# Attention a projected in narrower pieces, with its values made as token rows, under a new order of work

## What is computed

```
x = x + attn_a(layernorm(x))   # one head of width 128
x = x + ffn(layernorm(x))      # 512 x 512, int4 weights unpacked
x = x + attn_b(layernorm(x))   # 32 heads of width 16, rotary, causal
x = x + ffn(layernorm(x))      # the same weights

attn_a(x): q, k, v = split(x @ Wqkv + bqkv)         # Wqkv is 512 x 384
           a = softmax(q @ k.T / sqrt(128))
           return (a @ v) @ Wo + bo
```

## Time and profile before

| | |
|---|---|
| time, median of 3 runs (range) | 273.23 us (272.33 to 276.82) |
| the profiled execution: its time, its span | 273.97 us, 272.2 us |
| PE busy | 254.4 us, 93% |
| DVE busy | 224.4 us, 82% |
| POOL busy | 182.2 us, 67% |
| ACT busy | 145.0 us, 53% |
| PE's granted clock | 1.000 |

### The profile page before, as it was taken

One profiled execution on the slowest core, in us unless ns is written; L12 is line 12 of the kernel. 1 busy time (PEld: TensorE's weight loads), 2 busy tenths in 40 slices (PEclk: granted clock), 3 DMA queues, 4 the chain that ended last, 5 costly groups with the idle time before them and its releaser, 6 DMA issues.

```text
span 272.2 us, 6539 instructions
## 1 busy us (share of the span) xinstructions
PE 254.4 (93%) x2363; PEld 213.5 (78%) x2363; DVE 224.4 (82%) x402; ACT 145.0 (53%) x239; POOL 182.2 (67%) x229
## 2 busy tenths in 40 slices
PE   7699999998989999999899999997999999999964
PEld 2597887896888987888798898885868876785744
DVE  3682679497798989899888899987988999966976
ACT  2749996644546073457443478526433683268030
POOL 5578978998798495954858587495665552475070
PEclk9999999999999999999999999999999999999999
DMA  7998170203454336334333533531634531102012
GB/s 214 294 392 297 36 198 4 77 2 94 140 147 140 92 91 168 109 88 112 103 113 108 149 94 94 146 107 45 182 111 122 158 87 52 40 3 79 31 68 98
DMA packets 51192, 31.86 MB, mean 117 GB/s; under 512 B 5400, under 2 KB 46552, under 8 KB 51160
## 3 DMA queue, kind: packets, MB, share of 16 engines
q1 hardware_dynamic: 51160, 31.44, 38.8%
HBM read 22.91 MB, written 8.39 MB: 115 GB/s over the span
## 4 chain that ended last, share of the span: by engine, by line
PE 30%; POOL 16%; SPq 15%; DVE 14%; issue 9%; ACT 8%; DMA 7%; DVEq 0%; ACTq 0%; POOLq 0%
SPq L490 13%; PE psum L885 5%; PE psum L886 5%; PE psum L887 5%; PE psum L1052 3%; POOL rstd L543 3%; DVE stats L759 3%; PE psum L1037 3%; DMA QK<-qk_parts 3%; DMA qk_parts<-parts 2%; POOL X L556 2%; DVE XT_lo L764 2%; ACT E L718 2%; PE psum L1015 2%; POOL SH L576 2%
## 5 line engine op out<-in xcount | busy, mean ns | idle before, releaser
L588 POOL TENSOR_SCALAR_AFFINE_SELECT E<-E 128x512 f32<-128x512 f32 x64 | 40.7, 661 | 36.8 <-ACT E L718 36.8
L718 ACT ACTIVATE E<-psum 128x1536 f32<-128x1536 f32 x32 | 46.4, 1449 | 26.3 <-PE psum L1039 19.5
L838 DVE TENSOR_REDUCE nmax<-psum 128x4 f32<-128x512 f32 (+1 forms) x64 | 59.1, 939 | 0.7 <-PE psum L1015 0.6
L885 PE MATMUL psum<-XT_lo,wb_hi 128*128 128x256 f32 x128 | 37.7, 294 | 0.0
L886 PE MATMUL psum<-XT_hi,wb_lo 128*128 128x256 f32 x128 | 36.2, 283 | 0.0
L887 PE MATMUL psum<-XT_hi,wb_hi 128*128 128x256 f32 x128 | 36.1, 282 | 0.0
L622 ACT ACTIVATE XN<-X,offset,rstd 128x512 f32<-128x512 f32 x30 | 24.1, 809 | 19.6 <-POOL offset L544 19.5
L764 DVE TENSOR_TENSOR XT_lo<-psum,XT_hi 128x512 fp32r<-128x512 f32 x32 | 21.5, 683 | 15.6 <-ACT XT_hi L595 15.5
L595 ACT ACTIVATE parts<-SH 128x512 bf16<-128x512 f32 x32 | 19.9, 626 | 25.4 <-POOL SH L581 14.1
L885 PE MATMUL psum<-wb_lo,XT_hi 128*128 128x256 f32 (+1 forms) x96 | 32.6, 339 | 0.0
L1015 PE MATMUL psum<-QK 128*128 128x128 bf16 x256 | 28.8, 220 | 3.1 <-DMA QK<-qk_parts 3.1
(11 more groups left out here) (104 smaller groups left out, 677.5 us busy)
## 6 DMA issues: line engine op xcount, KB each, us to landing
QK<-qk_parts SPq DMA_DIRECT2D x192, 64.0 KB
qk_parts<-parts SPq DMA_DIRECT2D x16, 384.0 KB, 2.8
X<-L_attn_a_x SPq DMA_DIRECT2D x8, 256.0 KB, 4.7
out<-X SPq DMA_DIRECT2D x6, 256.0 KB, 2.4
...
wb_raw<-L_attn_b_wk SPq DMA_DIRECT2D x1, 1024.0 KB, 11.4
wb_raw<-L_attn_b_wv SPq DMA_DIRECT2D x1, 1024.0 KB, 11.9
...
```

The source lines that it names most:

```text
L588: last = nc.gpsimd.affine_select(out=e, in_=e, compare_op=ALU.is_ge, fill=0.0, base=0, pattern=[[0, GH], [1, P]], channel_multiplier=-1)
L718: nc.scalar.activation(E[:, n % 2], bank(3, 3), ACT.Exp, scale=float(HD) ** -0.5).then_inc(done[k], 1)
L838: nc.vector.tensor_reduce(nmax[:, u % 2, g::NG, t], (bank(1, 2) if t else bank(0)).rearrange("p (h k) -> p h k", h=GH), AX, ALU.max, negat ...
L885: nc.tensor.matmul(out_, stat[0], mov[1], start=first, stop=False)
```

## The change

- `Wqkv` comes in three loads of 256 KB: q, k, v. `QH` and `QL` become two steps each, one for q and one for k. The bias of q and k is loaded as two columns, and that of v as 128 channels broadcast to all partitions (`bias_v`), a load of its own.
- Batch 0 is projected by `QP` in six steps instead of `QK` and `QV`: `("QP", t, i)` is token half t of q (i = 0), k (1) or v (2). Each is 4 x 3 = 12 matmuls of 128 moving columns. A step needs only its own half of the tokens and its own part of the weight.
- `QV` for batches 1 to 3 now takes the tokens as the stationary operand and the v weight as the moving one: 2 x 4 x 3 = 24 matmuls of 128 columns. `QK` stays as it was for those batches.
- `VC`, `VA` and `AC` are gone. A new DVE step `VB` reads the product in PSUM, adds the bias row and writes `va`, which has two slots.
- `PLAN` is a new list throughout, and 9 `KP` matmuls stand at the start instead of 14. All steps not named here are the same in kind and number.

The list, its beginning only:

```diff
-    ("D", "x", 0, 1), ("LN", 1, 0, 1), ("D", "x", 0, 0), ("D", "x", 1, 0), ("D", "x", 1, 1), ("RS", 1, 0, 1),
-    ("KP", 14), ("NO", 1, 0, 1), ("LN", 1, 0, 0), ("RS", 1, 0, 0), ("T", 1, 0, 1), ("D", "wqkv", 1), ("LN", 1, 1, 0),
-    ("VH",), ("D", "x", 2, 0), ("NO", 1, 0, 0), ("D", "wqkv", 0), ("D", "bqkv"), ("LN", 1, 1, 1), ("RS", 1, 1),
-    ("D", "x", 2, 1), ("T", 1, 0, 0), ("TH", 1, 0, 1), ("NO", 1, 1, 0), ("VL",), ("TL", 1, 0, 1), ("T", 1, 1, 0),
-    ("TH", 1, 0, 0), ("QH",), ("TL", 1, 0, 0), ("QS",), ("D", "bias_o"), ("QL",), ("BA", 1, 0, 0), ("TH", 1, 1, 0),
-    ("QV", 0), ("NO", 1, 1, 1), ("T", 1, 1, 1), ("TH", 1, 1, 1), ("QK", 0), ("VC", 0), ("TL", 1, 1, 0), ("VA", 0),
-    ("LN", 1, 2, 1), ("TL", 1, 1, 1), ("QC", 0), ("QV", 1), ("LN", 1, 2, 0), ("RS", 1, 2), ("D", "q"), ("NO", 1, 2, 1),
-    ("DQ",), ("BA", 1, 1, 1), ("SA", 0), ("AM", 0), ("BA", 1, 0, 1), ("AC", 0), ("NO", 1, 2, 0), ("AE", 0), ("QK", 1),
-    ("WT", 0), ("VC", 1), ("WT", 3), ("QC", 1), ("D", "x", 3, 1), ("LN", 1, 3, 1), ("D", "x", 3, 0), ("LN", 1, 3, 0),
-    ("ET", 0), ("EC", 0), ("T", 1, 2, 1), ("WC", 3), ("WC", 0), ("D", "ww", 0), ("TH", 1, 2, 1), ("T", 1, 2, 0),
-    ("OA", 0), ("D", "zs"), ("SA", 1), ("TL", 1, 2, 1), ("OC", 0), ("WH", 0, 1), ("BA", 1, 2, 1), ("TH", 1, 2, 0),
-    ("TL", 1, 2, 0), ("AI", 0), ("D", "wo1"), ("BA", 1, 1, 0), ("WT", 2), ("WA", 0, 0), ("AM", 1), ("WT", 1), ("WC", 1),
 ...
+    ("D", "x", 0, 0), ("LN", 1, 0, 0), ("RS", 1, 0, 0), ("NO", 1, 0, 0), ("D", "x", 0, 1), ("LN", 1, 0, 1),
+    ("D", "bqkv"), ("QS",), ("D", "x", 1, 1), ("D", "x", 1, 0), ("RS", 1, 0, 1), ("LN", 1, 1, 1), ("KP", 9),
+    ("D", "wqkv", 0), ("QH", 0), ("D", "wqkv", 1), ("LN", 1, 1, 0), ("T", 1, 0, 0), ("TH", 1, 0, 0), ("QL", 0),
+    ("NO", 1, 0, 1), ("T", 1, 0, 1), ("D", "bias_o"), ("QH", 1), ("RS", 1, 1), ("TL", 1, 0, 0), ("QP", 0, 0), ("QL", 1),
+    ("TH", 1, 0, 1), ("TL", 1, 0, 1), ("D", "wqkv", 2), ("BA", 1, 0, 1), ("D", "x", 2, 0), ("D", "x", 2, 1),
+    ("LN", 1, 2, 1), ("LN", 1, 2, 0), ("VH",), ("NO", 1, 1, 1), ("QP", 0, 1), ("D", "x", 3, 1), ("VL",), ("QP", 1, 0),
+    ("T", 1, 1, 1), ("D", "q"), ("NO", 1, 1, 0), ("TH", 1, 1, 1), ("TL", 1, 1, 1), ("T", 1, 1, 0), ("TH", 1, 1, 0),
+    ("QP", 1, 1), ("D", "x", 3, 0), ("QC", 0), ("QP", 0, 2), ("D", "bias_v"), ("BA", 1, 0, 0), ("QP", 1, 2),
+    ("LN", 1, 3, 1), ("RS", 1, 2), ("NO", 1, 2, 1), ("SA", 0), ("TL", 1, 1, 0), ("QK", 1), ("D", "ww", 1),
+    ("LN", 1, 3, 0), ("NO", 1, 2, 0), ("D", "wo1"), ("RS", 1, 3), ("T", 1, 2, 0), ("AM", 0), ("AE", 0), ("TH", 1, 2, 0),
 ...
-READ_BY = {"WT": "WC", "T": "TL", "QK": "QC", "QV": "VC", "SA": "AE", "VA": "AC", "ET": "EC", "OA": "OC", "WA": "WD",
+READ_BY = {"WT": "WC", "T": "TL", "QK": "QC", "QP": "QC", "QV": "VB", "SA": "AE", "ET": "EC", "OA": "OC", "WA": "WD",
            "F": "FD", "PJ": "RO", "VP": "VV", "MT": "M2", "PV": "NA", "WO": "OD"}
 
 
@@ -252,9 +253,14 @@
             continue
         if k not in READ_BY or (k in PAIRS and st[2]) or (k == "WO" and st[3]):
             continue
+        if k == "QP" and st[1:] not in ((0, 0), (0, 2)):
+            continue
         bank = pool[turn % len(pool)]
         turn += 1
         bank_of[st], before[st] = bank, owner[bank]
+        if k == "QP":
+            owner[bank] = ("VB" if st[2] == 2 else "QC", 0)
+            continue
         owner[bank] = (READ_BY[k], *(st[1:2] if k in PAIRS else st[1:3] if k == "WO" else st[1:]))
     return bank_of, before
 
@@ -271,7 +277,7 @@
         s, b, t = st[1:] if st[0] == "T" else (5, *st[1:3])
         slot = (b % 2, b % 2, 2, 0, 1)[s - 1]
         slot_of[st], before[st] = slot, readers.get((slot, t), [])
-        readers[slot, t] = {1: [("QK", b), ("QV", b)], 2: [("F", 2, b, t)], 4: [("F", 4, b, t, 1) if b == B - 1 else ("F", 4, b, t)],
+        readers[slot, t] = {1: [("QK", b), ("QV", b)] if b else [("QP", t, i) for i in range(3)], 2: [("F", 2, b, t)], 4: [("F", 4, b, t, 1) if b == B - 1 else ("F", 4, b, t)],
                             5: [("WO", b, t, 1)],
                             3: [("PJ", 4 * b + m, 1) for m in range(KT)] + [("VP", 2 * b + i, 1) for i in range(2)]}[s]
     return slot_of, before
@@ -345,8 +351,8 @@
         minus_half = sb("minus_half", [P, NT], F32)
         bqkv_c = sb("bqkv_c", [P, 4], F32)
         qkT = sb("qkT", [P, 2, 2, S], F32)
-        vT = sb("vT", [P, S], F32)
-        va = sb("va", [P, NT, DA], F32)
+        va = sb("va", [P, 2, NT, DA], F32)
+        bias_v = sb("bias_v", [P, DA], F32)
         EA = sb("EA", [P, NT, S], F32)
         ETs = sb("ETs", [P, NT, S], F32)
         OTa = sb("OTa", [P, S], F32)
@@ -434,8 +440,10 @@
                     elif what == "wqkv":
                         sp.dma_start(wqkv_raw[:, :, part_of[st[2]]], rows(Wqkv)[:, :, part_of[st[2]]]).then_inc(here, 16)
                     elif what == "bqkv":
-                        sp.dma_start(bqkv_c[:, 0:3], bqkv.rearrange("(j p) -> p j", p=P), allow_slow_non_contiguous=True
+                        sp.dma_start(bqkv_c[:, 0:2], bqkv[0:2 * DA].rearrange("(j p) -> p j", p=P), allow_slow_non_contiguous=True
                                      ).then_inc(here, 16)
+                    elif what == "bias_v":
+                        sp.dma_start(bias_v[:], bqkv[2 * DA:3 * DA].partition_broadcast(P)).then_inc(here, 16)
                     elif what == "bias_o":
                         sp.dma_start(bias_o[:], bo.partition_broadcast(P)).then_inc(here, 16)
                     elif what == "q":
@@ -636,29 +647,18 @@
                     b = st[1]
                     act.wait_ge(loaded["bqkv",], 16)
                     act.wait_ge(done["QS"], 1)
-                    act.wait_ge(done["QK"], upto("QK", b))
+                    if b:
+                        act.wait_ge(done["QK"], upto("QK", b))
+                    else:
+                        act.wait_ge(done["QP"], last_of(*[("QP", t, i) for t in range(NT) for i in range(2)]))
                     if b >= 2:
                         act.wait_ge(done["SA"], upto("SA", b - 2))
-                    ps = bank(bank_of["QK", b])
+                    ps = bank(bank_of["QK", b] if b else bank_of["QP", 0, 0])
                     for i in range(2):
                         last = nc.scalar.activation(qkT[:, b % 2, i], ps[:, i * S:(i + 1) * S], ACT.Identity,
                                                     bias=bqkv_c[:, (3, 1)[i]:(4, 2)[i]],
                                                     scale=1.0 if i else float(DA) ** -0.5)
                     last.then_inc(done[k], 1)
-                elif k == "VC":
-                    b = st[1]
-                    act.wait_ge(loaded["bqkv",], 16)
-                    act.wait_ge(done["QV"], upto("QV", b))
-                    if b:
-                        act.wait_ge(done["VA"], upto("VA", b - 1))
-                    nc.scalar.activation(vT[:], bank(bank_of["QV", b])[:, 0:S], ACT.Identity, bias=bqkv_c[:, 2:3]
-                                         ).then_inc(done[k], 1)
-                elif k == "AC":
-                    b = st[1]
-                    act.wait_ge(done["VA"], upto("VA", b))
-                    if b:
-                        act.wait_ge(done["OA"], upto("OA", b - 1))
-                    copy(va[:].rearrange("p t d -> p (t d)"), bank(bank_of["VA", b])[:, 0:NT * DA]).then_inc(done[k], 1)
                 elif k == "AE":
                     b = st[1]
                     act.wait_ge(done["AM"], upto("AM", b))
@@ -737,9 +737,9 @@
                     link(nc.vector.tensor_scalar(w[:, :, :, 1], q_int[:], 15, None, ALU.bitwise_and))
                     nc.vector.tensor_copy(w_f[:], w_int[:]).then_inc(done[k], 1)
                 elif k == "QL":
-                    dve.wait_ge(done["QH"], 1)
-                    nc.vector.tensor_tensor(wqkv_lo[:, :, part_of[0]], wqkv_raw[:, :, part_of[0]],
-                                            wqkv_hi[:, :, part_of[0]].bitcast(F32), ALU.subtract).then_inc(done[k], 1)
+                    part = part_of[st[1]]
+                    dve.wait_ge(done["QH"], upto("QH", st[1]))
+                    nc.vector.tensor_tensor(wqkv_lo[:, :, part], wqkv_raw[:, :, part], wqkv_hi[:, :, part].bitcast(F32), ALU.subtract).then_inc(done[k], 1)
                 elif k == "QS":
                     dve.wait_ge(loaded["bqkv",], 16)
                     nc.vector.tensor_scalar(bqkv_c[:, 3:4], bqkv_c[:, 0:1], float(DA) ** -0.5, None, ALU.mult
@@ -779,6 +779,18 @@
                     b = st[1]
                     dve.wait_ge(done["AE"], upto("AE", b))
                     nc.vector.reciprocal(inv_a[:, b % 2], sum_a[:, b % 2]).then_inc(done[k], 1)
+                elif k == "VB":
+                    b = st[1]
+                    dve.wait_ge(loaded["bias_v",], 16)
+                    if b:
+                        dve.wait_ge(done["QV"], upto("QV", b))
+                    else:
+                        dve.wait_ge(done["QP"], last_of(*[("QP", t, 2) for t in range(NT)]))
```

(69 more changed lines are left out.)

## The result

The changed kernel takes 286.24 us (median of 6 runs, 284.37 to 290.21), the kernel before 272.69 us (median of 6, 272.21 to 276.82): a ratio of 1.0475 (95% interval 1.0436 to 1.0514), **13 us slower**, where 279.0 was forecast with 286 as the upper end.

What follows compares the result with a forecast made beforehand. PE was taken to bound the kernel until 51.35 us. Narrow matmuls +7.3, v transposes -0.9 and earlier start -0.9 gave +5.5 us, 279.0 us; own range 275.5 to 283, with rivals 270 to 286.

Steps and rivals of the forecast that it cites:

- What bounds the kernel: PE is full from 11.4 to 51.3 us; what it does more or less there moves everything after it.
- the landmark: First matmul of ("PJ", 0, 0) on PE, also first PJ: 51.35 us before, forecast to move +5.7 us to 57.0.
- PE streams without pause: In the opening's full stretch, matmul spacing is proportional to columns: 0.118 us for 256, 0.23 for 512.
- The price of a narrow matmul: Three-pass matmuls of 128 columns cost 0.11 us from weight loads: 144 come (15.8), 72 wide go (8.5), +7.3 us.
- The bounds of 0.059 and 0.218 us: Narrow matmul's limits: lower if only columns count, upper if the fp32r form is no faster than plain float32.
- The start: First QP on PE at 10.5 us against 11.43, -0.9 us; a late bias load before QS could make it +0.2.
- I put it at nothing, and at 1 us if the loads slow down as well: Opening on PE: cost if the first QP, after nine KP instead of 14, ran at 1.2 GHz.
- After that PE should not wait: Behind the first QP, low weights and token halves are ready before PE needs them; no wait costed.
- the new order: Changed step order behind the first PJ was costed at nothing, with 2 us to either side.
- The range: Own range 275.5 to 283 us, from narrow-matmul pace, QS, clock and order; 270 to 286 with rivals.
- loads were not hidden: Rival for narrow matmuls: weight loads hidden, only columns count, -1.8 us, 271.4 us; chance 0.13.
- the fast form does not end below 256 columns: Rival for narrow matmuls: fast form ends below 256 columns, 0.218 us each, +21 us, 294 us; chance 0.15.

Runs made afterwards that it cites:

- e8: Kernel before, only q and k of batches 1 to 3 made in 128-column halves (144 narrow matmuls for 72 wide): 278.64 us, ratio 1.0218.
- e7: Kernel before, values made as token rows for batches 1 to 3 only (72 narrow matmuls for 36 wide): 278.74 us, ratio 1.0177.
- e10: Kernel before, values of all four batches as token rows, 10 more KP filling PE's idle gaps in the opening: 277.84 us, ratio 1.0196.
- e1: Changed kernel with 14 opening KP matmuls instead of 9, nothing else: 281.40 us, ratio to the kernel before 1.0278.
- e2: Kernel before with 9 opening KP matmuls instead of 14: 275.58 us, ratio 1.0081.
- e9: Changed kernel with 14 KP and 8 more KP after the first transposes, where PE is idle: 280.41 us, ratio to the kernel before 1.0278.
- e4: Changed kernel with 9 KP, q and k of batch 0 again one step of 256-column matmuls: 281.39 us, ratio to the kernel before 1.0299.
- e6: Changed kernel with 14 KP, the v weight's rounding moved behind the two XN of batch 1: 284.89 us (278.55 to 289.68), no ratio given.
- e12: Changed kernel with 14 KP, 8 more filling the gap, v weight's rounding behind the two XN of batch 1: 279.90 us, ratio to before 1.0268.
- e5: Changed kernel's new order with 14 KP, all projections wide, values made the old way: 278.64 us, ratio to the kernel before 1.0192.

## Why the prediction was wrong

**What bounds the kernel: right.** PE's full stretch carried everything added to it to the end; 12.0 us at the landmark are 11.4 us of span. Only "PE streams without pause" was a little too strong: short pauses of some 0.7 us in the kernel before take up that much of an added cost (e8).

**The price of a narrow matmul: right.** 0.111 us at 2.4 GHz against the 0.11 taken, and the steps of e8 give 7.4 us where it gives 7.5. The three runs that isolate it moved first PJ by 3.05 (e7), 6.5 (e8) and 3.7 us (e10) where it gives 3.1, 7.5 and 4.3: the right size, with the pauses taken up. The bounds of 0.059 and 0.218 us were both off. The rule of the Trainium skill, "TensorE: Matmul & The Clock Gate", section "LDWEIGHTS (loading the stationary operand)", 107 ns for 128 columns, fits that spacing at 2.4 GHz, and not the 0.213 us at 1.2 GHz; the 81 ns of its section "Back-to-back issue gap" fit neither.

**The start: right.** The first `QP` began at 10.32 us, 10.5 forecast; in e1 it was 9.98. `QS` ran at 5.2 us, so the bias load was no obstacle.

**The step that failed: "I put it at nothing, and at 1 us if the loads slow down as well".** The sentence before it had seen that some of the 14 `KP` ran at 1.2 GHz. It missed that the nine kept are just those at 1.2 GHz: 4.02 us for nine, 0.45 each, where the fourteen took 5.02. And it took a load of 0.11 us to be the same at either level, so that 128 columns would stream behind it unseen. The loads come 0.213 us apart at 1.2 GHz. Nor did I ask for how long. For the wide matmuls of e2 it was 3 us, for the narrow ones 11. In the changed kernel 44 narrow matmuls (10.32 to 21.2 us) at 0.213 instead of 0.111 us are 4.5 us, and eight transposes 0.7 (19.62 - 18.04 = 1.58 against 0.87 at 28.23 us in the same trace): **5.2 us, where nothing or 1 us was put**. At the landmark e1 is 4.4 us sooner than the changed kernel: the 5.2, and 0.3 for an earlier start, less 1.2 for the wait below, which is hidden while PE is slow. With the level held and the gap filled (e9), the time is 280.4, 5.0 us below the changed kernel's 285.4.

**A second step: "After that PE should not wait".** I followed the halves of batch 0 and the low weights, but not ACT's next step. `VH` waits for the third weight load, with the two XN of batch 1 behind it: 1.2 us of PE in e1, hidden in the changed kernel. And the new order was costed at nothing only behind the landmark, and not at all ahead of it: there the XN of stage 3 comes 1.2 us late in the changed kernel, in e1, e4, e6, e9 and e12. Why DVE is that late with its sums, no run tells.

**The sum, mended.** Landmark of the changed kernel: 7.5 for the narrow matmuls, -0.7 for three `VA`, -1.1 for the start, +5.2 for the clock and +1.2 for the wait ahead of stage 3: +12.1 us, 12.0 measured. With the clock held: 7.5 - 0.7 - 1.4 and the two waits of 1.2, +7.8 us; e1 has 59.0 - 51.35 = 7.6. **Past the landmark** nothing was won or lost, within the 2 us allowed; as other kernels vary there by as much, that it came out so close is partly luck. **The range** was added up wrongly too: its terms, at their ends, give 276.3 to 284.5, not 275.5 to 283. The rivals were not what happened: loads were not hidden, and the fast form does not end below 256 columns, although the first 11 us look just like it, 0.213 us at a bound of 0.218. The change at 21.2 us, at equal form, tells the clock from the form, and e1 does so by its single edit.

**What stays open.** Whether the narrow matmuls alone, behind a dense opening, could bring the level down in a longer stretch: 24 in a row (e7) and 48 (e8) did not. Why the narrow stream stayed at 1.2 GHz for 11 us, while wide ones left that level after 3 to 4, the runs show only as a fact of one profile each. And what the new order costs by itself: e5 leaves 1.2% to 2.7%.
